# A four-layer graph network on one core: the second layer's dense work placed inside its pass over the edges

## What is computed

```python
xn = layernorm(x)
# graph part
self_part = xn @ W1.T                       # 3125x256
proj = xn @ W2.T                            # 3125x256
nb = segment_sum(proj[src], dst)            # 50000 rows gathered, summed by destination
# mixing part: linear attention with 8 heads of 32
q, k, v = split(xn @ w_qkv + b_qkv)         # per head
k, v = ln(k) * kg + kb, ln(v) * vg + vb     # over the 32 channels of a head
kv = k.T @ v / N                            # per head, over all nodes
ret = q @ kv + xn
h = gelu(ret @ w1 + b1)
x = x + relu(self_part + nb) + h @ w2 + b2 + xn
```

## Time and profile before

| | |
|---|---|
| median of three runs | 9663.89 us |
| the profiled execution, own time | 9673.63 us |
| its span in the trace | 9671.9 us |
| TensorE, VectorE, ScalarE, GpSimd busy over the span | 54%, 56%, 20%, 39% |
| mean granted clock of TensorE | 0.781 |
| layer 1 from the end of its norm to the next layer's norm | 1018.7 us |

### The profile page before, as it was taken

One profiled execution on the slowest core, in us unless ns is written; L12 is line 12 of the kernel. 1 busy time (PEld: TensorE's weight loads), 2 busy tenths in 40 slices (PEclk: granted clock), 3 DMA queues, 4 the chain that ended last, 5 costly groups with the idle time before them and its releaser, 6 DMA issues. The chain is left out here.

```text
span 9671.9 us, 114565 instructions
## 1 busy us (share of the span) xinstructions
PE 5212.6 (54%) x21955; PEld 3844.8 (40%) x21956; DVE 5460.1 (56%) x12451; ACT 1976.8 (20%) x4673; POOL 3732.0 (39%) x3791
## 2 busy tenths in 40 slices
PE   3551454545565545644924454907666676665443
PEld 3551333333344523324813344803444434443243
DVE  5884555656663244464155554144888648885743
ACT  0000333133301100011212211201444124441111
POOL 0884566076501347500136620221655115550003
PEclk9999776767776866676967775958899788887767
DMA  1333333133304623301723311922666136661025
GB/s 56 127 127 41 98 105 99 31 104 101 88 6 140 209 77 88 75 7 59 279 58 84 82 34 51 305 57 90 183 185 186 40 105 183 181 183 47 5 72 168
DMA packets 585603, 1020.35 MB, mean 105 GB/s; under 512 B 187333, under 2 KB 352810, under 8 KB 576714
## 3 DMA queue, kind: packets, MB, share of 16 engines
q0 software_dynamic: 191616, 489.64, 19.4%
q1 hardware_dynamic: 363275, 496.15, 15.6%
q10 hardware_dynamic: 30528, 32.52, 1.0%
HBM read 927.10 MB, written 90.26 MB: 105 GB/s over the span
## 5 line engine op out<-in xcount | busy, mean ns | idle before, releaser
L663 POOL DMA_INDIRECT l_hgt_ep_g<-l_hgt_tkm,l_hgt_ep_ix x832 | 931.5, 1120 | 655.4 <-PE l_hgt_ep_out L739 446.3
L663 POOL DMA_INDIRECT l_gat_ep_g<-l_gat_th,l_gat_ep_ix x832 | 927.5, 1115 | 433.0 <-issue 234.0
L739 PE MATMUL l_hgt_ep_out<-l_hgt_ep_g,l_hgt_ep_here 128*126 128x288 f32 x1664 | 587.9, 508 | 511.4 <-DVE l_hgt_ep_g L874 311.1
L739 PE MATMUL l_gat_ep_out<-l_gat_ep_g,l_gat_ep_here 128*126 128x264 f32 x1664 | 626.5, 536 | 64.0 <-issue 30.0
L739 PEld LDWEIGHTS l_hgt_ep_out<-l_hgt_ep_g,l_hgt_ep_here 128*126 128x126 f32 x1664 | 364.8, 230 | 680.9 <-issue 577.8
L459 POOL DMA_INDIRECT recs<-place_stage,place_pos x400 | 520.4, 1301 | 288.7 <-issue 284.1
L663 POOL DMA_INDIRECT l_ep_g<-l_table,l_ep_ix x416 | 410.8, 987 | 233.6 <-issue 119.7
L1718 POOL IOTA f_moe_route_io<- 1x56 f32 (+2 forms) x4 | 0.7, 166 | 1289.8 <-ACTq L92 1289.8
L1907 DVE TENSOR_TENSOR f_moe_experts_yb<-f_moe_experts_py,f_moe_experts_b2s 128x256 f32<-128x256 f32 x208 | 88.4, 425 | 725.5 <-PE f_moe_experts_py L1890 694.1
L1055 PE MATMUL l_sum_out<-l_sum_g,l_sum_here 128*125 128x256 f32 x832 | 336.7, 540 | 290.4 <-DVE l_g L1080 121.9
L739 PEld LDWEIGHTS l_gat_ep_out<-l_gat_ep_g,l_gat_ep_here 128*126 128x126 f32 x1664 | 414.9, 264 | 188.2 <-issue 61.7
(11 more groups left out here) (575 smaller groups left out, 12169.7 us busy)
## 6 DMA issues: line engine op xcount, KB each, us to landing
l_hgt_ep_hot<-locrow SPq DMA_DIRECT2D x208, 256.0 KB
f_moe_experts_w1b<-in_L_ffn_w SPq DMA_DIRECT2D x32, 1024.0 KB
f_moe_experts_w2b<-in_L_ffn_w SPq DMA_DIRECT2D x32, 1024.0 KB
f_moe_experts_w1b<-in_L_ffn_w SPq DMA_DIRECT2D x64, 512.0 KB
f_moe_experts_w2b<-in_L_ffn_w SPq DMA_DIRECT2D x64, 512.0 KB
f_moe_experts_w1b<-in_L_ffn_W SPq DMA_DIRECT2D x56, 512.0 KB
f_moe_experts_w2b<-in_L_ffn_W SPq DMA_DIRECT2D x56, 512.0 KB
l_gat_ep_hot<-locrow SPq DMA_DIRECT2D x104, 256.0 KB
```

The lines of the kernel that those rows point to most:

```text
L663: gp.indirect_dma_start(g[:, b % 4, j, 0:W], None, table, bass.IndirectOffsetOnAxis(ap=ix[:, b, j:j + 1].bitcast(U32), axis=0)).then_inc(s ...
L739: pe.matmul(out[:, t % 4, 0:WO], here[:, b % 2, t, :], g[:, b, t, F:F + WO], start=True, stop=True).then_inc(s_out, 1)
```

## The change

`edge_sums` is gone. `layer1` is written anew as two blocks.

The first block (`l1_pre`) transposes xn once and keeps the result, `xt` [128, 25, 2, 125], for the whole layer. For each block of nodes TensorE multiplies it with both weight matrices (512 columns in two PSUM banks); VectorE copies the rows for the table, SyncE stores them, and ScalarE copies the self part into the accumulator, which therefore isn't cleared any more. All weights of the layer are loaded here. The mean over each head of 32 columns is subtracted from the weights and the bias of k and v, so that k and v come out with mean zero.

The second block (`l1_edges`) has 106 steps, one for each group and two more. Its ring of gathered rows has eight groups instead of four. TensorE, ScalarE and VectorE are unrolled into straight code with fixed buffer numbers; GpSimd keeps its loop. Beside the group's products and additions, steps carry parts of the dense work of one block of nodes: `kv_at` places the 25 blocks' k and v, norm and gram over steps 1 to about 50, and `out_at` places q, the residual, up, Gelu and down over steps 56 to about 105. The chain of small matmuls lies between.

Cut to its core:

```diff
-def edge_sums(core, name, acc, table, idx):
...
-        g = ph.sb("g", [128, 4, EG, D])
...
-                if later(i, 4):
-                    gp.wait_ge(s_out, EG * (i - 3))
...
-        edge_sums(core, "l1_sum", g, table, core.e_src)
-        with Phase(core, "l1_v") as pw:
-            w = weights(core, pw, "w", D, ins["L1_gnn_W1T"])
-            project(core, "l1_self", xn, w, D, ("add", g))
...
-            linear_mix(core, "l1_mix", xn, g, "copy", D, 32, 1.0 / N, ins["L1_mix_kv"], ins["L1_mix_WqT"], None,
...
-            project(core, "l1_up", g, w, D, ("copy", h), bias=b1)
-            on_scalar(core, "l1_gelu", lambda act: act.activation(h[:, :, :], h[:, :, :], ACT.Gelu))
-            project(core, "l1_down", h, w2, D, ("add", x), bias=b2)
-        add_to(core, "l1_bias", x, xn)
+            head_mask(core, "l1_mask", mask, 32, 1.0 / N)
...
+            @block.tensor
+            def _(pe):
+                for i in range(NT + 2):
+                    if i < NT:
+                        if i >= 2:
+                            pe.wait_ge(s_xt, i - 1)
+                        for k in range(2):
+                            mm = pe.transpose(pt[:, i % 2, P * k:P * k + P], xn[:, i, 128 * k:128 * k + 128], core.ident[0:P, 0:P])
...
+                        for h in range(2):
+                            for k in range(2):
+                                mm = pe.matmul(out[:, t % 2, h, 0:D], xt[:, t, k, :], wp[:, k, D * h:D * h + D], start=k == 0, stop=k == 1)
...
+        with Phase(core, "l1_edges") as pe_:
+            RB = 8
...
+            SPAN = 46
+            kv_at = {1 + SPAN * t // NT: t for t in range(NT)}
+            out_at = {56 + SPAN * t // NT: t for t in range(NT)}
...
+                def indices(i, b):
+                    if later(i, RB):
+                        gp.wait_ge(s_out, EG * (i - RB + 1))
+                    gp.tensor_copy(ix[:, b, :], core.e_src[:, bass.ds(i * EG, EG)]).then_inc(s_ix, 1)
...
+            @block.tensor
+                for i in range(NG + 2):
...
+                            pe.matmul(out[:, j, 0:D], here[:, i % 4, j, :], g[:, i % RB, j, :], start=True, stop=True).then_inc(s_out, 1)
+                    if i in kv_at:
...
+                        for k in range(2):
+                            mm = pe.matmul(side[0:P, 0, :], xt[:, t, k, :], wkv[:, k, :], start=k == 0, stop=k == 1)
...
+                    if i in out_at:
...
+                                mm = pe.matmul(side[:, 0, P * r:P * r + P], a[:, k, 128 * r:128 * r + 128], xt[:, t, k, :], start=k == 0, stop=k == 1)
...
+            @block.vector
+                for i in range(NG + 2):
+                    if i + 1 < NG:
+                        edges_here(i + 1)
+                    if 1 <= i <= NG:
+                        add(i - 1)
+                    if i - 1 in kv_at:
+                        t = kv_at[i - 1]
+                        v.wait_ge(s_kv, t + 1)
...
+                        v.tensor_tensor(y[:, t % 4, :], side[0:P, 0, :], bkv[:, :], ALU.add).then_inc(s_y, 1)
+                        v.tensor_tensor(x[:, t, :], x[:, t, :], xn[:, t, :], ALU.add)
+                    if i - 2 in kv_at:
...
+                        v.tensor_reduce(ve[:, t % 4, :], sq[:, t % 2, :].rearrange("p (h c) -> p h c", c=32), AX.X, ALU.add)
+                        v.drain()
+                        v.tensor_scalar(ve[:, t % 4, :], ve[:, t % 4, :], 1.0 / 32, 1e-5, ALU.mult, ALU.add).then_inc(s_ve, 1)
+                    if i - 3 in kv_at:
...
+                        v.reciprocal(sd[:, t % 4, :], sd[:, t % 4, :])
+                        v.drain()
+                        v.tensor_tensor(y3, y3, sd[:, t % 4, :].unsqueeze(2).to_broadcast([P, 16, 32]), ALU.mult)
+                        v.drain()
+                        v.tensor_tensor(y[:, t % 4, :], y[:, t % 4, :], gain[:, 0, :], ALU.mult)
+                        v.drain()
+                        v.tensor_tensor(y[:, t % 4, :], y[:, t % 4, :], gain[:, 1, :], ALU.add).then_inc(s_ln, 1)
...
+                    if i - 1 in out_at:
...
+                            o = v.scalar_tensor_tensor(out=ret[:, t % 2, r, :], in0=side[:, 0, P * r:P * r + P], scalar=cvec[:, r:r + 1], in1=xt[:, t, r, :],
+                                                       op0=ALU.add, op1=ALU.add)
...
+                    if i - 4 in out_at:
...
+                        v.tensor_tensor(x[:, t, :], x[:, t, :], side[0:P, 3, 0:D], ALU.add).then_inc(s_x, 1)
+                v.wait_ge(s_added, TE)
+                v.drain()
+                v.scalar_tensor_tensor(out=x[:, :, :], in0=acc[:, :, :], scalar=0.0, in1=x[:, :, :], op0=ALU.max, op1=ALU.add)
```

More of the change, by code:

```diff
@@ L1015, in _ @@
                 put(t)
-def edge_sums(core, name, acc, table, idx):
-    nc = core.nc
-    with Phase(core, name) as ph:
-        ix = ph.sb("ix", [128, 8, EG], I32)
-        g = ph.sb("g", [128, 4, EG, D])
[L1025 to L1037, removed]
-                if later(i, 4):
-                    gp.wait_ge(s_out, EG * (i - 3))
[L1040 to L1082, removed]
@@ L1998, in layer1 @@
 def layer1(core, x, xn):
-    ins = core.ins
+    nc, ins = core.nc, core.ins
     normalize(core, "l1_norm", x, xn)
@@ L2002, in layer1 @@
     with Phase(core, "l1") as ph:
[L2003 to L2006, removed]
-        edge_sums(core, "l1_sum", g, table, core.e_src)
-        with Phase(core, "l1_v") as pw:
-            w = weights(core, pw, "w", D, ins["L1_gnn_W1T"])
-            project(core, "l1_self", xn, w, D, ("add", g))
-        def relu_add(v):
-            v.scalar_tensor_tensor(out=x[:, :, :], in0=g[:, :, :], scalar=0.0, in1=x[:, :, :], op0=ALU.max, op1=ALU.add)
@@ L2014, in layer1 @@
[L2014 to L2022, removed]
+        acc = ph.sb("acc", [P, NT, D])
+        xt = ph.sb("xt", [128, NT, 2, P])
+        wkv = ph.sb("wkv", [128, 2, 512])
@@ L2025, in spread @@
                                   small[:, i:i + 1, :].to_broadcast([P, 8, 32]))
-            on_vector(core, "l1_spread", spread)
-            linear_mix(core, "l1_mix", xn, g, "copy", D, 32, 1.0 / N, ins["L1_mix_kv"], ins["L1_mix_WqT"], None,
-                       kv_b=(ins["L1_mix_kv_b"],), q_b=ins["L1_mix_q_b"],
-                       prepare=lambda kv: normalize(core, "l1_kvn", kv, kv, G=16, gain=gain))
-        add_to(core, "l1_ret", g, xn)
-        with Phase(core, "l1_h") as ph2:
-            h = ph2.sb("h", [P, NT, D])
-            w = weights(core, ph2, "w", D, ins["L1_mix_w1"])
-            w2 = weights(core, ph2, "w2", D, ins["L1_mix_w2"])
-            b1 = rowvec(core, ph2, "b1", D, ins["L1_mix_b1"], parts=P)
-            b2 = rowvec(core, ph2, "b2", D, ins["L1_mix_b2"], parts=P)
-            project(core, "l1_up", g, w, D, ("copy", h), bias=b1)
-            on_scalar(core, "l1_gelu", lambda act: act.activation(h[:, :, :], h[:, :, :], ACT.Gelu))
-            project(core, "l1_down", h, w2, D, ("add", x), bias=b2)
@@ L2040, in layer1 @@
-        add_to(core, "l1_bias", x, xn)
+                g3 = wkv[:, :, :].rearrange("p k (h c) -> p (k h) c", c=32)
+                m3 = means[:, :, :, :].rearrange("p k h o -> p (k h) o")
+                b3 = bkv[:, :].rearrange("p (h c) -> p h c", c=32)
+                v.tensor_reduce(m3, g3, AX.X, ALU.add)
+                v.tensor_reduce(bmeans[:, :, :], b3, AX.X, ALU.add)
+                v.drain()
+                v.scalar_tensor_tensor(out=g3, in0=m3.to_broadcast([128, 32, 32]), scalar=-1.0 / 32, in1=g3, op0=ALU.mult, op1=ALU.add)
```

223 lines of the change are left out of this document (added).

## The result

The changed kernel took 9355.08 us (median of four runs) against 9676.9 for the kernel before in the same rounds, ratio 0.967, 95% interval 0.9631 to 0.9709. It is faster by 322 us; the forecast was 9395 and 269. The profiled execution took 9376.83 us, its span is 9375.0.

The account below looks back on a forecast made before the run. The prediction took GpSimd's gathers, held up by late VectorE additions, to bound the edge pass. 63 + 680 + 7 = 750 us replaces 1018.7, so 9673.6 becomes 9405, or 9395 as median; likeliest 9340 to 9450, wider 9265 to 9510.

Parts of the forecast that it names:

- the narrow range: Whole program: likeliest times, 9340 to 9450 us, with the pass at 630 to 740; chance 0.60.
- First block: Layer 1 ahead of the edge pass: the new block takes 63 us against 41.5, ends 58 and 75.
- Relu and sum: After the pass: one instruction over all blocks, 6.83 us, and a barrier; 7 us together.
- What is removed: Layer 1 behind the edge pass: all 355.9 us of stages go, including both projects' staging copies and repeated transposes.
- The pass: Layer 1's edge pass: 46 k and v steps at 6.93, 46 output steps at 6.2, 12 at 5.88; 680 us in all.
- It costs about half of what is put under it.: Edge pass: each us more of VectorE work costs 0.56, 0.46 or 0.41 us, by comparing four passes.
- Only its wait for a free slot now stands ahead of the index copy, with nothing else behind it.: GpSimd's queue in the pass: same 416 gathers and 104 copies, no cost counted for the new order.
- GpSimd's least: Edge pass: gathers 412.1, index copies 22.6 and issue gaps 104.9 make 539.6 us, the least the pass can take.
- Signals that arrive late under a dense stream of gathers: Old edge pass: late signals between engines delay VectorE's additions, one by 3.2 us; GpSimd waits some 71 us at the full ring.
- Rival 1: Edge pass: GpSimd alone sets it at 550 us, since late additions no longer reach it; time 9265, chance 0.15.
- Rival 2: Edge pass: VectorE bounds the k and v half, 9 us a step; pass 780, time 9495; chance 0.20 shared with another rival.
- The ring of eight: Edge pass: the deeper ring saves only the first groups' 5 us; bounds nothing and all of GpSimd's 71 us.

Follow-up runs that it names:

- the old kernel with the copy behind: Kernel before the change, with only GpSimd's index copy moved directly ahead of its own group's gathers, ring of four: 9624.25 us, ratio 0.9989 (first kind).
- the copy ahead: Changed kernel with GpSimd's index copy issued one group ahead of its gathers again: 8958.77 us, ratio 0.9656 (second kind); 9316.24 us, ratio 0.9671 (first).
- the one-hot with one input: Changed kernel, index copy one group ahead, each group's one-hot made by four VectorE instructions with one SBUF tensor input: 9352.09 us, ratio 0.97.
- the two with pauses: The changed kernel (9355.08 us) and the old kernel with the copy behind (9624.25 us); in both the index copy stands directly ahead of its gathers.
- packing: Changed kernel with index copy one group ahead and k and v half in 25 steps, not 46: 9346.11 us, ratio 0.9696 (first kind).

## Why the prediction was right, and where its steps failed

The time (9355 for 9395) was inside the narrow range, the gain 322 us for 269. By the prediction's own steps:

- **First block**, 63 us: 62.3. **Relu and sum**, 7: 7.5. **What is removed**, 355.9: all gone, and nothing but the relu and the next norm stands behind the pass. These three are right.
- **The pass**, 680: 619.9 + 15.4 = 635.3 us. This is the term that was mis-sized, by 45. The k and v half ran at 6.0 us a group and not 6.93, the output half at 5.9 and not 6.2. The tail of 10 was 15. VectorE's load was not the error: 4.2 us a group in the k and v half where 4.5 was reckoned, 2.6 in the other where 2.9 was.
- **"It costs about half of what is put under it."** This step failed. The slopes of 0.56, 0.46 and 0.41 came from passes that differ in more than VectorE's load. On the second kind of chip the third layer's pass, with 0.79 us a group more on VectorE than layer 1's, is 9.2 us longer in all, 0.09 a group. GAT's is another 50.2 us longer, but there GpSimd itself works 50.3 us more (485.85 for 435.53). The experiment without the dense work gives 18 us for 123 us of VectorE (355.6 less 232.6), one part in seven, and most of it is GpSimd's gathers getting longer. It was not run on the first kind; the nearest pair there, the old kernel with the copy behind (609.2) and the changed one (619.9), differs by 10.7 us with the dense work, ring and form of the code together, and its gathers alone by 10.8 (405.3 for 416.1).
- **"Only its wait for a free slot now stands ahead of the index copy, with nothing else behind it."** This step failed too: costed at nothing, it is 104 gaps of 0.76 us in place of 0.16, 62 us of GpSimd's queue. GpSimd's least was no longer 539.6 but some 602, before the longer gathers.
- **Signals that arrive late under a dense stream of gathers.** The reading of the earlier trace rows fits this kind of chip, and is not a property of the kernel. On the first kind, GpSimd got on at 5.87 to 5.94 us a group in the versions whose own queue needs less, by way of stops (the kernel before, the copy ahead, the one-hot with one input), and at 5.86 and 5.96 without stops in the two with pauses. On the second kind it goes at its own 5.3.
- **Why GpSimd had no stops in the profile after**, although it was expected to wait: additions were still late, as forecast, but its own queue needs 5.96 us a group, about the pace that this kind of chip showed in the other versions with evenly spread work. So the 62 us of the copy order cost 9 in the gathers where the prediction was tested (619.9 against 610.9), and 64 where the chip is of the second kind (621.4 against 557.7).
- **Rival 1** had the right engine, since GpSimd alone sets the pass, but at 5.96 us and not 5.2. Its 540 us of gathers was approached, with 557.7, only in the old copy order on the other kind of chip. **Rival 2** is what packing makes of it: 81% of VectorE and 7.1 us a group. **The ring of eight**, 5 us credited: nothing on the second kind; on the first it did not remove the stops of the version with the copy ahead.
- **The Trainium skill's** rule from "SBUF — State Buffer", section "Who interferes with whom", is that a VectorE instruction with two SBUF inputs contends with a GpSimd instruction that reads SBUF. The prediction's estimate from it was at most some 60 us on GpSimd's least. The trace agrees with its direction: without the added instructions the gathers are 16 us shorter in all, and an index copy, usually 0.19 us, takes 0.57 beside a one-hot. The measured price is about a quarter of that.
- **Luck.** The time lay in the range because the range was wider than the error, not because the cover had its price right. With the cover at nothing the prediction's own sum gives 611.3 + 10 for the pass and 9336, nearer to 9355 than 9395 was. And the copy order, which it left out, costs 64 us of gathers on the other kind of chip where it cost 9 here.

What stays open is why the signals are late on the one kind of chip. The gathered rows arrive there as promptly (in the kernel before, the last packet of rows of a gather ends 1.4 us after the instruction by the median, on either kind); the lateness lies between an instruction's end and the engine that waits for it. A ring of four with the dense work wasn't run on that kind, nor the kernel before with a ring of eight.

The version with the copy ahead beats both kernels on the second kind (0.9656 against the changed kernel's 0.9733 of the kernel before) and comes out level with the changed one on the first (0.9671 and 0.967).

## What to carry to other kernels

When an engine sets the pace of a loop, add up its whole queue from the trace, waits for itself included, before and after every reordering: an instruction whose result the same engine needs next costs the round trip (0.6 us more here) each time, and a step of prefetch takes it away. Idle engines beside such a pace-setter can carry dense work cheaply (here 18 us for 123 of VectorE) until one of them needs longer in a step than it does; spread the work evenly. And don't take a slope from passes that differ in several ways, nor a stall without a visible cause for a property of the program, until it was seen on a second chip.

## What the runs showed of the hardware

- Two kinds of chip: the same program took 9596 to 9707 us on some and 9247 to 9298 on others, 4%. Most of the difference lies in passes with a dense stream of gathers: GAT's first 694.8 against 605.4 us, layer 1's 611.3 against 546.0, the third layer's 655.9 against 555.2. HGT's, where gathers are further apart, took 811.9 against 810.5. A change can be worth 314 us on one and 252 on the other.
- On the first kind the pass settles at 5.9 us a group whether GpSimd pauses 0.6 us more at each group or runs at 5.2 to 5.4 and stops for 1 to 6 us, mostly at every third to seventh.
- A GpSimd gather takes 0.95 us, and often 1.2 to 1.4 when it lies across a VectorE instruction with two SBUF inputs. Of the 416 gathers 41 were over 1.1 us in the first profile before, 56 in the one after and 53 with the copy ahead on the second kind; every one of them lies across such an instruction (the one-hot, x plus xn, or the three steps on y), and none without one is over 1.0. In the version with the copy ahead it looks like this:

```profile
3341.50 0.69 DVE L2208 TENSOR_TENSOR l_edges_y<-l_edges_y,l_gain 125x512 f32<-125x512 f32 x1
3341.82 1.19 POOL L2080 DMA_INDIRECT l_edges_g<-l_table,l_edges_ix  x1 [0.30 <-issue]
3342.26 0.69 DVE L2210 TENSOR_TENSOR l_edges_y<-l_edges_y,l_gain 125x512 f32<-125x512 f32 x1
3342.87 0.67 DVE L2170 TENSOR_TENSOR l_edges_here<-keep_iota,keep_e_loc 128x500 f32<-128x500 f32 x1
3343.02 0.57 POOL L2074 COPY l_edges_ix<-keep_e_src 128x4 int32<-128x4 int32 x1
```
